# State times decay moves from VectorE to ScalarE in a chunked state-space scan

## The reference, cut to what matters

```python
decay = jnp.exp(dt_t * a)[..., None, None]
state = decay * state + b_bar[..., None] * x_t[:, :, None, :]
y_t = jnp.einsum('bhn,bhnp->bhp', c_t, state)
```

## Time and profile before

| | |
|---|---|
| median of 3 runs | 1240.99 us (1229.99 to 1241.63) |
| profiled execution: its own time | 1237.72 us |
| its span | 1235.9 us |
| DVE busy / ACT busy / POOL busy in it | 1044.4 / 650.9 / 774.8 us |

### The profile page before, as it was taken

One profiled execution on the slowest core, in us unless ns is written; L12 is line 12 of the kernel. 1 busy time (PEld: TensorE's weight loads), 2 busy tenths in 40 slices (PEclk: granted clock), 3 DMA queues, 4 the chain that ended last, 5 costly groups with the idle time before them and its releaser, 6 DMA issues.

```text
span 1235.9 us, 34852 instructions
## 1 busy us (share of the span) xinstructions
PE 1189.5 (96%) x13979; PEld 984.0 (80%) x13979; DVE 1044.4 (85%) x2024; ACT 650.9 (53%) x1406; POOL 774.8 (63%) x726
## 2 busy tenths in 40 slices
PE   8999999999999989999999998999999999999998
PEld 4666667888888878787877787788888888899998
DVE  7999867999997988999999987987777766777676
ACT  6999975444445434443443344545545543554453
POOL 4889855445455567666666657466666654576774
PEclk9999999999999999999999999999999999999999
DMA  9798754533343433343433336564454545799994
GB/s 296 264 339 346 289 212 130 127 134 123 133 134 126 135 129 116 118 133 122 135 114 121 117 134 193 175 145 83 95 113 91 105 86 117 241 320 329 339 328 167
DMA packets 122448, 214.83 MB, mean 174 GB/s; under 512 B 22448, under 2 KB 80560, under 8 KB 117552
## 3 DMA queue, kind: packets, MB, share of 16 engines
q1 hardware_dynamic: 109136, 195.32, 46.3%
q0 software_dynamic: 12288, 17.05, 8.1%
q10 hardware_dynamic: 864, 0.24, 0.1%
HBM read 131.03 MB, written 81.53 MB: 172 GB/s over the span
## 4 chain that ended last, share of the span: by engine, by line
PE 57%; DVE 28%; issue 6%; DMA 2%; ACT 2%; POOL 2%; SPq 1%; DVEq 0%; ACTq 0%; POOLq 0%
PE ps L1415 10%; PE ps L1779 10%; PE ps L2289 7%; PE ps L2268 7%; PE ps L2053 6%; DVE decay L1050 5%; DVE spare L1019 5%; PE ps L2055 3%; DVE b_w L1117 2%; DVE ystat L1161 2%; PE ps L1494 2%; PE ps L1427 2%; PE ps L682 2%; PE ps L630 1%; DVE yb L1089 1%
## 5 line engine op out<-in xcount | busy, mean ns | idle before, releaser
L1365 ACT ACTIVATE decay<-tap,ncum 128x64 f32<-128x64 f32 x344 | 87.1, 335 | 159.7 <-POOL tap L1266 159.7
L1963 POOL DMA_INDIRECT ffn_dram<-ob,idx x64 | 107.9, 1686 | 86.5 <-DVE ob L1882 70.8
L1294 POOL TENSOR_SCALAR yb<-x,dcol 128x512 f32<-128x512 f32 x64 | 46.5, 727 | 125.1 <-DVE ystat L1161 78.8
L1271 POOL TENSOR_TENSOR x_lo<-x,x_hi 128x512 fp32r<-128x512 f32 x56 | 72.6, 1297 | 80.0 <-ACT x_hi L1344 80.0
L2053 PE MATMUL ps<-dn,mid_hi 128*128 128x512 f32 x288 | 104.9, 399 | 0.5 <-DVE moments L1853 0.5
L2011 ACT ACTIVATE mid<-ps,b_up 128x512 f32<-128x512 f32 x96 | 65.8, 689 | 67.1 <-PE ps L1779 62.3
L1415 PE MATMUL ps<-x_hi,w_hi_b 128*128 128x512 f32 x240 | 99.9, 416 | 0.0
L2144 POOL TENSOR_SCALAR yc<-yc,gn_scale,gn_shift 128x512 f32<-128x512 f32 x56 | 77.2, 1391 | 30.4 <-DMA yc<-y_dram 30.4
L1415 PE MATMUL ps<-x_lo,w_hi_b 128*128 128x512 f32 x240 | 94.6, 394 | 0.7 <-issue 0.7
L1415 PE MATMUL ps<-x_hi,w_hi_c 128*128 128x512 f32 x240 | 95.1, 396 | 0.0
L1415 PE MATMUL ps<-x_lo,w_hi_c 128*128 128x512 f32 x240 | 93.7, 390 | 0.0
(11 more groups left out here) (329 smaller groups left out, 3931.0 us busy)
## 6 DMA issues: line engine op xcount, KB each, us to landing
x_dram<-x SPq DMA_DIRECT2D x16, 1024.0 KB, 5.4
yc<-y_dram SPq DMA_DIRECT2D x16, 1024.0 KB, 6.7
y_dram<-yb SPq DMA_DIRECT2D x30, 512.0 KB, 3.3
x<-x_dram SPq DMA_DIRECT2D x26, 512.0 KB, 3.8
tap<-cum_half_dram SPq DMA_DIRECT2D x86, 128.0 KB, 3.0
tap<-cum_dram SPq DMA_DIRECT2D x86, 128.0 KB, 3.0
rows_dram<-xn SPq DMA_DIRECT2D x16, 512.0 KB, 3.3
ffn_dram<-zero SPq DMA_DIRECT2D x64, 128.0 KB
```

The source lines that it names most:

```text
L1271: nc.gpsimd.tensor_tensor(x_lo[b % 2][:, m, :], x2[b % NX][:, m, :], x_hi[b % 2][:, m, :].bitcast(F32), ALU.subtract).then_inc(x_lo_ready, 1)
L1365: n = nc.scalar.activation(decay[g % 2][:, h, :], key_row[g % NR][:, h, :], ACT.Exp, bias=t.ncum[:, g, h:h + 1])
L1963: pool.indirect_dma_start(out=t.ffn_dram, out_offset=bass.IndirectOffsetOnAxis(ap=t.idx[:, e, h * HC + c:h * HC + c + 1], axis=0), in_=ob[ ...
```

## The change

shrink leaves DVE's program and enters ACT's. DVE used one tensor_tensor of 128x256 with the decay broadcast along 64 columns. ACT uses four activations (Copy) of 128x64, one per pair of heads, each with a column of dec as its scale; only the last raises the semaphore. On ACT shrink(g, 0) stands ahead of decays(g + 1), and shrink(g, 1) behind decays(g + 1) and ahead of x_hi. DVE keeps the additions (L1060, L1065) and waits for ACT's count before each. At g = 0 and g = 32 there is no shrink(g, 0), at g = 31 and g = 63 no shrink(g, 1).

```diff
+    def shrunk(g, j):
+        return (2 * SPAN - 2) * (g // SPAN) + 2 * (g % SPAN) + j
...
-        def shrink(g, j):
-            source = (states[g % 2], state_mid)[j]
-            n_scaled[0] += 1
-            dve.wait_ge(state_ready, ends(g)) if j == 0 else dve.wait_ge(mid_ready, g + 1)
-            v.tensor_tensor(state_tmp, source, dec[j][:, g, :].unsqueeze(2).to_broadcast([P, MT, HD]),
-                            ALU.mult).then_inc(scaled, 1)
...
-                dve.wait_ge(scaled, n_scaled[0])
+                dve.wait_ge(scaled, shrunk(g, 0))
                 v.tensor_tensor(state_mid, ps_new[0], state_tmp, ALU.add).then_inc(mid_ready, 1)
...
-            dve.wait_ge(scaled, n_scaled[0])
+            dve.wait_ge(scaled, shrunk(g, 1))
             v.tensor_tensor(states[(g + 1) % 2], ps_new[1], state_tmp, ALU.add).then_inc(state_ready, 1)
...
-            if not first:
-                shrink(g, 0)
...
-            if not last:
-                shrink(g, 1)
             v.tensor_tensor(mix.rearrange("p (a h) n -> p a (h n)", a=2), ps_scores,
...
+        def shrink(g, j):
+            source = (states[g % 2], state_mid)[j]
+            if j == 0:
+                act.wait_ge(state_ready, ends(g))
+            else:
+                act.wait_ge(mid_ready, g + 1)
+            for m in range(MT):
+                n = nc.scalar.activation(state_tmp[:, m, :], source[:, m, :], ACT.Copy, scale=dec[j][:, g, m:m + 1])
+            n.then_inc(scaled, 1)
...
+            if g % SPAN:
+                shrink(g, 0)
             if g + 1 < NT:
                 decays(g + 1)
+            if g % SPAN < SPAN - 1:
+                shrink(g, 1)
             if b + 2 < NB:
                 hi_part(b + 2, c)
```

More of the change, by code:

```diff
@@ L1100, in add_other_halves @@
             n.then_inc(y_ready, 1)
-        n_scaled = [0]
         def begin():
```

## The result

| | before | changed |
|---|---|---|
| median of 4 runs | 1240.95 us | 1280.47 us (1276.05 to 1280.96) |
| ratio of changed to before, 95% interval | | 1.033 (1.027 to 1.039) |
| profiled execution, its span | 1237.72, 1235.9 us | 1280.23, 1278.4 us |

What follows compares the result with a forecast made beforehand. DVE's round was taken to bound list and search chunks before; the change closes a ring of waits. 31.2 + 8.3 - 2.7 - 3.5 + 3.0 = +36.3 us on 1241.0 gave 1277 us, range 1245 to 1300.

Steps and rivals of the forecast that it cites:

- The ring: bn_stats, skip term, masks, decays, shrink(g, 1), end state, next bn_stats: 10.86 us per list chunk, 10.16 per search chunk.
- the open turn at g = 31: List chunks: no shrink(g, 1) at g = 31, so the closed path of waits is open for one turn; 2.0 us given back.
- The four activations: One shrink on ACT: 3 x 0.24 + 0.34 = 1.06 us, taken from the pitch of the eight exponentials.
- The rival with 0.34 us each: Slower still: activations with a pointer as scale don't overlap, 0.34 us each; 1291 us, chance 0.13.
- they can fall to PE's 34.1: Chunks 1 to 4: DVE's relief shows, from 36.9 us to PE's time; -2.7 us.
- I take -3.5 us: Chunks 15 to 23: gain from DVE's relief, between 0 and 5.2 us, with DVE staying near the bound.
- The end: End of the scan: shrink(61, 0) stands behind token_hi(1) on ACT, so PE's update of 62 is late; +3 us.
- No change: the digits escape: Rival: DVE's digits start before POOL's x_lo and take 0.68 us, list period 9.77 us; 1237 us, chance 0.11.
- Faster: Rival: the path of waits is slack, DVE only loses work and PE's 8.52 us rule; 1186 us, chance 0.10.
- the 1.27 us more of a list chunk are not PE's: List chunks before: 9.79 us against PE's 8.52 in a plain chunk, the excess read as DVE's round.
- The signs and the bounds: New profile: end state waits some 3 us (list), about 2 (search); skip term 0.86 us after bn_stats; PE waits 1.5 to 2.3.
- 1264 to 1289 by its own terms: Whole kernel, main forecast's span: activations 1.0 us and end 0, up to 1.1, +5 and no slot-chunk gain; chance 0.66.

Runs made afterwards that it cites:

- masks first: Changed kernel with GpSimd making the masks of g + 2 ahead of the skip term of chunk g; 1210.76 us, ratio to the kernel before 0.975.
- the other order on ScalarE: Changed kernel with shrink(g, 1) moved ahead of decays(g + 1) on ScalarE, behind shrink(g, 0); 1218.99 us, ratio to the kernel before 0.983.
- the control: Kernel before, both shrinks on VectorE, with GpSimd's masks ahead of the skip term; 1221.14 us, ratio 0.986.
- shrink(g, 0) alone: Kernel before with only shrink(g, 0) moved to ScalarE, shrink(g, 1) left on VectorE; 1228.06 us, ratio 0.990.
- both cures together: Changed kernel with shrink(g, 1) ahead of decays on ScalarE and GpSimd's masks ahead of the skip term; 1215.39 us, ratio to the kernel before 0.981.

## Why the prediction was right

The terms of the sum, with the starts of b_w in both profiles:

| stretch | before | after | difference | predicted |
|---|---|---|---|---|
| up to chunk 1 | 201.56 | 203.63 | +2.1 | 0 |
| chunks 1 to 4 | 36.87 | 38.97 | +2.1 | -2.7 |
| 10 search chunks | 93.27 | 101.31 | +8.0 | +8.3 |
| chunks 15 to 23 | 81.94 | 84.31 | +2.4 | -3.5 |
| 31 list chunks | 303.50 | 326.68 | +23.2 | +31.2 |
| end, to the last b_w (781.27, 822.64) | 64.13 | 67.74 | +3.6 | +3.0 |

Together +41.4 us, and the spans differ by 42.5; the predicted sum was +36.3.

The mechanism was right. That the time came within 3.5 us of the forecast is partly luck: the list row was predicted 8 us too long, and the rows at the start, in chunks 1 to 4 and in chunks 15 to 23 together 12.8 us too short.

- **The ring** was right, in its stations and in its size. The search turn hit to 0.03 us. The list turn was 0.26 us too long: list_values' second instruction takes 0.70 in place of 0.86 us (533.09 above; VectorE's shrink no longer stretches it), and shrink and its handing over 1.08 in place of 1.14. The first and last arc make the rest, 0.04. 31 x 0.26 = 8 us, all of the difference in that row. The 2.0 us given back for the open turn at g = 31 fit as a sum: 31 x 10.60 less the measured 326.7 is 1.9 (chunk 31 took 8.10 us, and two others about 0.5 too much).
- **The four activations**: 1.06 us was the right form of cost. The rival with 0.34 us each is refuted (0.24 each, 0.96 to the next instruction).
- **Up to chunk 1** nothing was predicted, and 2.1 us came. 0.9 of them lie ahead of the first b_w; 1.2 are chunk 0, where the end state at 203.29 waits 2.54 us for shrink(0, 1) behind decays(1).
- **The gains in the other stretches** were the failed terms, "they can fall to PE's 34.1" and "I take -3.5 us". Both stretches have a loss. Chunks 1 to 4 have no bn_stats in the ring, but the skip term isn't the only thing that makes ACT late: behind a wait of exp_rows and of the masks for the DMA of their row shrink(g, 0) and the decays come late as well. 1.9 of the 2.1 us are chunk 4 (8.49 before, 10.39 after), shown here behind two waits of chunk 1, timeline of DVE, with the row of ACT in between:

```profile
207.40 0.42 DVE L1056 TENSOR_TENSOR mix<-ps,decay 128x256 f32<-128x256 f32 x1 [0.93 <-ACT decay L1367]
...
210.27 0.42 DVE L1061 TENSOR_TENSOR state<-ps,decay 128x256 f32<-128x256 f32 x1 [1.85 <-ACT decay L1367]
...
233.26 0.64 ACT L1349 ACTIVATE ecum_row<-cum_row 128x512 f32<-128x512 f32 x1 [1.00 <-DMA cum_row<-cum_dram]
...
237.88 0.42 DVE L1061 TENSOR_TENSOR decay<-ps,decay 128x256 f32<-128x256 f32 x1 [1.53 <-ACT decay L1367]
```

  Behind 237.88 the update of the threshold takes 1.09 us beside x_lo, where it took 0.16 before.

  In chunks 15 to 23 I had taken the ring for 6.4 us, and DVE's relief did show in chunk 16 (1.9 us shorter). In chunk 19 it went through another station: the skip term waited for the store of the output and not for bn_stats, and VectorE's long slot work still stood behind the end state.

```profile
382.63 0.70 POOL L1284 TENSOR_SCALAR yb<-x,dcol 128x512 f32<-128x512 f32 x1 [4.24 <-DMA y_dram<-yb]
...
387.78 0.42 DVE L1061 TENSOR_TENSOR state<-ps,decay 128x256 f32<-128x256 f32 x1 [3.02 <-ACT decay L1367]
...
391.58 2.00 DVE L1017 CAST chosen<-spare 128x512 f32<-128x512 int32 x1
```

  The end state waits 3.02 us, the last conversion lasts 2.00 us (0.76 before), and the chunk takes 13.02 us in place of 10.42. Chunk 17 lost 1.6 us more.
- **The end**: the middle state of chunk 61 waits 2.72 us for shrink behind the experts' casts, as written; +3.6 for +3.0.
- **"No change: the digits escape"** didn't come: x_lo started at 538.81 and the digits at 538.91, GpSimd first by 0.10 us (0.13 estimated), and they took 1.72 us. The Trainium skill's rule ("SBUF — State Buffer", Who interferes with whom: the order of issue decides who blocks) agrees with these runs: 1.73 us with the digits 0.11 us behind x_lo (masks first, 619.38 and 619.49), and in the changed kernel itself chunk 23, which has no list addition ahead of its digits, shows the other order, DVE first by 0.23 us:

```profile
425.32 0.68 DVE L1023 TENSOR_TENSOR spare<-chosen,cst 128x512 bf16<-128x512 f32 x1
425.55 1.60 POOL L1261 TENSOR_TENSOR x_lo<-x,x_hi 128x512 fp32r<-128x512 f32 x1 [2.35 <-ACT x_hi L1334]
425.92 1.78 DVE L1023 TENSOR_TENSOR spare<-gateT,cst 128x512 bf16<-128x512 f32 x1
```

  Now x_lo is stretched, to 1.60 from 1.28 us, and the digits' first instruction isn't. But their second one, which starts while x_lo runs, takes 1.78 us in its place (0.68 at 540.56 in the steady turn). From the first of the digits to bn_stats it is 2.30 us there and 2.25 in the steady turn, so nothing is saved. This rival had a second fault, then: its 9.77 us leave out that the next VectorE instruction is caught. Both of the digits' instructions stayed at 0.68 us only where x_lo didn't overlap them at all: shown with shrink(g, 1) behind x_hi (x_lo ended 0.29 us ahead of them) and with the other order on ScalarE (it started 1.82 us behind them).
- **"Faster"**: its 1186 us has not been reached by any version. It asked for PE's 8.52 in list chunks; they have 0.34 us of list matmuls of their own, and 8.88 is the floor that was measured. The prediction's reading that "the 1.27 us more of a list chunk are not PE's" was off by those 0.34 to 0.36 us.
- A reading of the prediction that the control corrects: I took 9.79 us as VectorE's work. It was work and blocking, and the blocking could be moved without moving work.
- **The signs and the bounds.** The waits ahead of the end state came as written (3.1 us on average in 30 of the 31 list chunks, 1.65 in search chunks), and so did the 0.86 us from bn_stats to the skip term (0.85). PE's wait for b_w did not: 1.5 to 2.3 us were written, and it was 1.2 on average, 1.6 at most. "1264 to 1289 by its own terms" doesn't follow from the terms that are named there, which give about 1271 to 1284.

## What to carry to other kernels

An instruction that moves to an idle engine takes the wait of whatever stands ahead of it in that engine's queue. Before moving work, follow who releases that wait back to the engine that you relieve: if the path comes back to it, the sum of the path is the new period, however idle every engine is. Here the same two products cost 3.3% behind decays and came with a gain of 1.7% one place ahead of it. And a long mean duration of one instruction can be blocking by another engine: look at its minimum, and try the order before moving it.

## What the runs showed of the hardware

TensorE at times pauses in the middle of the update of a chunk, with nothing that the profile names as releaser, and the longest such pause was 3.42 us, with the other order on ScalarE. Timeline of PE, then windows (us from the start: length, busy time and count of PE, PEld, DVE, ACT, POOL, granted clock, DMA share, GB/s) ahead of the pause and behind it:

```profile
555.28 0.48 PE L1499 MATMUL ps<-x_dt,b_w 64*64 64x64 f32 x4 [3.42 <-issue]
```

```profile
545.00:551.00 6.00, 6.00 (x112) 4.99 (x113) 3.61 (x8) 5.56 (x20) 4.45 (x5) 1.00 0.47 131
556.40:561.20 4.80, 4.80 (x13) 3.83 (x12) 3.83 (x8) 3.31 (x13) 0.00 (x0) 0.50 0.31 109
```

Behind the pause the granted clock is 0.50 for some 5 us, 1.2 in place of 2.4 GHz, with the engine busy all the time: the projection matmuls have a pitch of 0.43 in place of 0.23 us. That one chunk took 15.34 us in place of 8.88, 6.5 us in a kernel whose runs spread over 8.7.

It isn't an accident of that one execution. The kernel before has such a pause (1.71 us at 455.80, granted clock 0.55 in the 3.2 us behind it), and so have the changed kernel (1.14 us at 597.42, then 0.53 for 3.6 us), shrink(g, 0) alone (2.77 us at 453.90, then 0.64 for 4.7 us) and both cures together (2.86 us at 447.82, then 0.64 for 4.8 us). In five kernels such a pause lies in chunk 28: before, with shrink(g, 0) alone, with both cures, behind x_hi (1.55 us at 465.30) and in the control (1.78 us at 449.78). That it comes back in the same chunk speaks for the program and against chance, but its size changes from version to version, and its cause is open. A difference of half a per cent between two versions can be one such pause.
